# All later products of x taken in the first batch's pauses, and three norms' steps moved to ScalarE

## The reference

```python
x = x + 0.5 * ffn(layernorm(x))        # ffn: sum of 8 chosen adapters, one 256x256 matrix and a bias
x = x + attn(layernorm(x))             # below
x = x + 0.5 * ffn(layernorm(x))
# attn(x): RWKV block
h  = layernorm(x, g1, b1); hh = time_shift(h)
xk, xv, xr = (h * tm + hh * (1 - tm) for tm in (tm_k, tm_v, tm_r))
rwkv = sigmoid(xr @ Wr) * wkv(decay, first, xk @ Wk, xv @ Wv)    # a scan over the 512 tokens
x  = x + rwkv @ Wo
h  = layernorm(x, g2, b2); hh = time_shift(h)
xck, xcr = (h * cm + hh * (1 - cm) for cm in (cm_k, cm_r))
return x + sigmoid(xcr @ Wcr) * (square(relu(xck @ Wck)) @ Wcv)  # hidden size 1024
```

## Time and profile before

| | us |
|---|---|
| median of 3 runs | 461.88 (461.78 to 462.07) |
| the profiled execution, its own time | 462.52 |
| its span in the profile | 460.7 |
| PE busy | 444.5 |
| DVE busy | 394.4 |
| ACT busy | 255.8 |
| POOL busy | 153.9 |

### The profile page before, as it was taken

The page is one execution under the profiler, slowest core; times in us unless marked ns, Lnnn a source line. Parts: engine busy times, 40 slices in busy tenths (PEclk is TensorE's granted clock), DMA queues, the critical chain, the costliest instruction groups (busy, mean ns, idle before and its releaser), DMA issues. The chain is left out here.

```text
span 460.7 us, 6181 instructions
## 1 busy us (share of the span) xinstructions
PE 444.5 (96%) x2120; PEld 352.8 (77%) x2120; DVE 394.4 (86%) x813; ACT 255.8 (56%) x416; POOL 153.9 (33%) x126
## 2 busy tenths in 40 slices
PE   8979989999999999999999999999999999999995
PEld 8755966588759885788668885788678885878884
DVE  3889989999999899989998899979998999866224
ACT  1138466944786267814795287906793387826500
POOL 1424051335141544045242444054332534032010
PEclk9999999999999999999999999999999999999999
DMA  6960001002001100012001200010001000000101
GB/s 213 360 228 2 0 1 46 0 2 91 1 0 48 63 29 1 0 46 92 1 0 46 92 1 1 1 46 1 0 1 46 0 2 0 33 15 1 46 1 46
DMA packets 15953, 18.51 MB, mean 40 GB/s; under 512 B 1066, under 2 KB 13618, under 8 KB 15922
## 3 DMA queue, kind: packets, MB, share of 16 engines
q1 hardware_dynamic: 14522, 17.05, 10.5%
q10 hardware_dynamic: 1400, 1.07, 0.8%
HBM read 13.92 MB, written 4.19 MB: 39 GB/s over the span
## 5 line engine op out<-in xcount | busy, mean ns | idle before, releaser
L379 PE MATMUL pair<-wcv_sb,kk 128*128 128x256 f32 x512 | 114.3, 379 | 0.0
L379 PEld LDWEIGHTS pair<-wcv_sb,kk 128*128 128x128 f32 x512 | 96.8, 190 | 12.6
L1012 POOL TENSOR_TENSOR rstd_x<-vare_x,nhalf 128x4 f32<-128x4 f32 (+1 forms) x25 | 29.7, 1189 | 102.1 <-DVE vare_x L679 101.2
L501 ACT ACTIVATE h<-pair,vec 128x512 f32<-128x512 f32 x16 | 11.6, 775 | 88.8 <-PE pair L265 88.8
L357 PE MATMUL pair<-xck_hi,wck_hi 128*128 128x512 f32 x128 | 56.2, 439 | 1.8 <-ACT kk L542 1.1
L361 PE MATMUL pair<-xck_lo,wck_hi 128*128 128x512 f32 x128 | 50.3, 393 | 0.0
L358 PE MATMUL pair<-xck_hi,wck_lo 128*128 128x512 f32 x128 | 50.0, 391 | 0.0
L542 ACT ACTIVATE kk<-pair 128x512 f32<-128x512 f32 x64 | 37.9, 592 | 15.5 <-PE pair L361 13.7
L1055 POOL TENSOR_SCALAR work<-work,lowest 128x512 f32<-128x512 f32 x16 | 26.6, 1662 | 59.0 <-DVE work L770 59.0
L546 ACT ACTIVATE kk<-kk 128x512 f32<-128x512 f32 x64 | 38.9, 635 | 0.8
L1032 POOL TENSOR_TENSOR x2b<-xs,bias_bc 128x512 f32<-128x512 f32 x15 | 19.2, 1281 | 51.5 <-DVE xs L883 51.5
(11 more groups left out here) (123 smaller groups left out, 918.5 us busy)
## 6 DMA issues: line engine op xcount, KB each, us to landing
x<-in_x_dram SPq DMA_DIRECT2D x8, 512.0 KB, 4.1
xt<-in_xt_dram SPq DMA_DIRECT2D x8, 512.0 KB, 5.3
out_dram<-xs SPq DMA_DIRECT2D x16, 256.0 KB, 2.1
work<-in_ffn_w_dram ACTq DMA_DIRECT2D x4, 256.0 KB, 3.8
work<-in_ffn_w_dram SPq DMA_DIRECT2D x4, 256.0 KB, 4.1
kk<-in_wck_dram SPq DMA_DIRECT2D x1, 1024.0 KB, 11.1
wcv_sb<-in_wcv_dram SPq DMA_DIRECT2D x1, 1024.0 KB, 12.6
wk_sb<-in_wk_dram SPq DMA_DIRECT2D x1, 256.0 KB, 9.3
```

The lines of the kernel that those rows point to most:

```text
L379: last = nc.tensor.matmul(bank_of("kv", e, i)[:, t % TB * C:(t % TB + 1) * C], kk[:, n, tok:tok + P], wcv_sb[:, n, :], start=n == 0, stop= ...
L1012: nc.gpsimd.tensor_tensor(dst, src, power, ALU.pow).then_inc(done, 1)
```

## The change

Eight things change at once.

- The products of x for batches 2 to 7 are taken in the head, where the warm products stood. Their transposed inputs are loaded early into tiles that are unused then (x2b, thc, both xs, and the two xt tiles again). ACT copies the products of these six batches from PSUM to SBUF (`keep_first`), and `add_first` reads them there.
- `stats_x(b)` for b of 2 and more leaves DVE. ACT sums along rows with `accum_out`: four passes for the means, four for the variances. They stand behind `residual_of(f)`.
- `norm_first` for batches 1 and later leaves DVE for ACT, as a scale and a shift; POOL computes the shift. It stands behind the second key relu.
- `mix_r` leaves DVE: ACT scales the difference, and POOL adds h1.
- On DVE `stats_x1(f + 1)` comes behind `key_input_rest(f)`, where before it came ahead of `mix_ck(f)`.
- norm1 and norma become one tile, normed; h1 and h2 become one tile, h.
- On PE, the turning of x1 comes after four key blocks (before: three), and that of xa in the middle of the third quarter of the values.
- On ACT, the key relu and square of block 5 come ahead of the exponentials, and `h1_of` behind relu 3 (before: relu 2).

```diff
+            load_xt(2)
             load_weight("wr", wr_sb[:, :, :], wr)
...
+            load_xt(3)
+            load_xt(4)
+            load_xt(5)
             load_weight("wcr", wcr_sb[:, :, :], wcr)
             load_weight("wcv", wcv_sb[:, :, :], wcv)
             load_x(2)
-            load_xt(2)
-            load_xt(3)
+            load_xt(7)
+            load_xt(6)
...
             turn_x1(0)
-            warm(3, 13)
+            first_product(2)
             front_k(0)
             front_v(0)
             front_r(0)
-            pe.wait_ge(q_done, 2)
-            warm(2, 47)
+            first_product(3)
+            first_product(4)
+            first_product(5)
             output_product(0)
-            pe.wait_ge(t1_done, 2)
-            warm(3, 14)
+            first_product(6)
             turn_xa(0)
-            warm(3, 11)
+            first_product(7)
             for e in range(B):
                 f = e + 1
-                channel_keys(e, (0, 1, 2))
+                channel_keys(e, (0, 1, 2, 3))
                 if has(f):
                     turn_x1(f)
-                channel_keys(e, (3,))
...
                     output_product(f)
-                if has(f + 1):
-                    first_product(f + 1, (0,))
                 channel_values(e, 1)
-                if has(f + 1):
-                    first_product(f + 1, (1,))
+                channel_values(e, 2, range(HB // 2))
                 if has(f):
                     turn_xa(f)
-                channel_values(e, 2)
+                channel_values(e, 2, range(HB // 2, HB))
...
+            def stats_x(b):
+                act.wait_ge(x_loaded[b % X1], 16 * (b // X1 + 1))
+                act.wait_ge(rstd_done["x"], b)
+                act.wait_ge(gated_done, 2 * (b - 1) + 2)
+                for t in range(NT):
+                    nc.scalar.activation(thr.rearrange("p h t -> p (h t)")[:, t * C:(t + 1) * C], x1[b % X1][:, t, :], ACT.Identity, scale=-ROOT / C,
+                                         accum_out=mean_x[:, t:t + 1]).then_inc(means_done, 1)
+                for t in range(NT):
+                    act.wait_ge(means_done, NT * (b - 2) + t + 1)
+                    last = nc.scalar.activation(e_v[:, t // TB, t % TB * C:(t % TB + 1) * C], x1[b % X1][:, t, :], ACT.Square, scale=ROOT, bias=mean_x[:, t:t + 1],
+                                                accum_out=var_x[:, t:t + 1])
+                last.then_inc(vars_done, 1)
+
+            def norm_first(b):
+                act.wait_ge(shiftb_done, b)
+                act.wait_ge(turneda, 2 * (b - 1) + 2)
+                for t in range(NT):
+                    last = nc.scalar.activation(normed[:, t, :], x1[b % X1][:, t, :], ACT.Identity, scale=rboth[:, t:t + 1], bias=shiftb[:, t:t + 1])
+                    if t % TB == TB - 1:
+                        last.then_inc(normed1, 1)
+
+            def keep_first(b):
+                for i in range(BANKS):
+                    act.wait_ge(y1_ps, 2 * b + (BANKS if b >= B - 2 else i + 1))
+                    nc.scalar.activation(tok_bank(y1s[b], i), bank3(bank_of("y1", b, i)), ACT.Copy).then_inc(y1s_done, 1)
...
+            def scaled_difference(f):
+                for c in range(CH):
+                    act.wait_ge(xk_done, 2 * f + c + 1)
+                    act.wait_ge(xv_done, 2 * f + c + 1)
+                    nc.scalar.activation(xr[:, c, :], xr[:, c, :], ACT.Identity, scale=V["tm_r"][:, c:c + 1]).then_inc(scaled_done, 1)
...
+                if has(f + 1):
+                    stats_x(f + 1)
+                if has(f):
                     h2_of(f)
...
             def bias_to_x(b):
-                pool.wait_ge(bn_done["x"], b + 1)
+                pool.wait_ge(*((bn_done["x"], b + 1) if b < 2 else (vars_done, b - 1)))
...
+            def mix_r(f):
+                for c in range(CH):
+                    pool.wait_ge(scaled_done, 2 * f + c + 1)
+                    nc.gpsimd.tensor_tensor(xr[:, c, :], xr[:, c, :], h1[:, c, 0:T], ALU.add).then_inc(xr_done, 1)
```

More of the change, by code:

```diff
@@ L31, in build @@
     X1 = 3
+    ROOT = C ** -0.5
     LAST = B - 1
+    EARLY = range(2, B)
     with ExitStack() as ctx:
@@ L71, in build @@
         xa = sb("xa", [P, NT, C])
-        norm1 = sb("norm1", [P, NT, C])
-        norma = sb("norma", [P, NT, C])
+        normed = sb("normed", [P, NT, C])
         thc = sb("thc", [P, NT, C])
         x2b = sb("x2b", [P, NT, C])
+        y1s = {b: sb(f"y1s_{b}", [P, NT, C]) for b in range(2, B - 2)}
         kinds = ("x", "x1", "xa", "x2")
@@ L266, in turn, with to_tokens @@
                     last.then_inc(filled, 1)
-            def to_tokens(stage, src, w, signal, b, filled, part=range(BANKS)):
-                for i in part:
-                    take(pair_of(stage, b), i, signal, 2 * b + i + 1)
+            def to_tokens(stage, src, w, signal, b, filled, first=0):
+                for i in range(BANKS):
+                    take(pair_of(stage, b), i, signal, 2 * (b - first) + i + 1)
                     for t in range(TB):
@@ L308, in ffn_setup, with first_product @@
                 warm(3, 2)
[L310 removed]
+            def first_product(f):
                 if f == 0:
                     pe.wait_ge(s_ffn, 1)
[L313 to L314 removed]
+                pe.wait_ge(xt_loaded[f], 16)
+                if f in EARLY:
+                    to_tokens("y1", xt_of[f], ffn_t, y1s_done, f, y1_ps, first=EARLY[0])
+                else:
+                    to_tokens("y1", xt_of[f], ffn_t, x1_done, f, y1_ps)
             def turn_x1(f):
[L317 removed]
+                turn("turn_x1", normed, h1_done, f, normed1, turned1)
             def front(name, f, src, w, ready, signal, filled):
@@ L373, in channel_values @@
                     pe.wait_ge(s_wcv, 1)
-                if t % TB == 0:
+                if t % TB == 0 and 0 in part:
                     take(PAIR["kv"], i, kvs_done, 2 * e + i + 1)
-                for n in range(HB):
+                for n in part:
                     if t == 0:
@@ L380, in channel_values @@
                                             start=n == 0, stop=n == HB - 1)
-                if t % TB == TB - 1:
+                if t % TB == TB - 1 and HB - 1 in part:
                     last.then_inc(kv_ps, 1)
@@ L435, in _ @@
                     front_v(f)
-                channel_keys(e, range(some, HB))
+                channel_keys(e, (6, 7))
                 if has(f):
@@ L1076, in _ @@
             pool.wait_ge(s_decay, 2)
+            mix_r(0)
             hold_exponents(0)
```

122 lines of the change are left out of this document (70 added, 52 removed).

## The result

The changed kernel takes 478.64 us (median of 4 runs, 477.19 to 480.46), the kernel before 461.86 (461.78 to 462.07) on the same chip. The ratio is 1.0365, with a 95% interval of 1.0324 to 1.0405: slower by some 17 us, where 19 were forecast. The profiled execution took 480.46, the longest of the four.

What follows compares the result with a forecast made beforehand. PE bounded the loop (51.06 us an iteration); after the change a 53.7 us ring through the norm of x1 would. 77.6 + 322.2 + 80.0 = 479.8, with 1.8 around it 481.6 profiled, 481.0 median; range 459 to 491.

Steps and rivals of the forecast that it cites:

- a ring through the norm of x1: Loop chain through ACT, PE, DVE and POOL back to that norm: 47.3 us before, 53.7 after, above PE's 51.06.
- Six rings: Iterations 0 to 5, each taking a first product's sum, at 53.7 us each: 322.2.
- Span: Start at 77.6, six rings of 322.2 and an end of 80.0: 479.8 us, with 1.8 more around it.
- Piece 3: Key product to output product on PE: 24.3 less one key block of 1.4, so 22.9; rwkv 22.1 behind, hidden.
- Piece 5: POOL's root for the norm of xa waits behind ACT's eight sums: 1.1 us more, between 0.3 and 2.7.
- rival of dear sums: ACT's sums along rows cost 0.2 more for each of eight, rings 1.6 longer: 490.6 us; chance 0.18 (486 and above).
- Piece 6: Norm of xa to statistics of x1, with DVE's adds colliding with POOL's x1 + xa: 10.6 us.
- three of them wait until 4.1: Three of DVE's adds of x1 wait for POOL's 2.36 us sum and end at 5.2 behind the norm's start.
- no collision: DVE's adds and POOL's sum do not collide, ring 50.9: 464.2 us median; chance 0.19 (461 to 470).
- Piece 7: Statistics to norm of x1: statistics 2.2, negm 0.3, root 1.45, shift 0.4, so 4.4 us.
- PE stays the bound: Ring in truth 6 us shorter, so all PE loses is gained: 439.6 us median; chance 0.09 (under 455).

Runs made afterwards that it cites:

- e2: Changed kernel with the norm of x1 back on DVE, behind the mix of xcr: 463.67 us, ratio 1.0052 to the kernel before.
- e7: Changed kernel plus seven warm products of the identity ahead of the key product of batch 1: 478.88 us, ratio 1.0376 to the kernel before.
- e6: As e5, but with mix_r left on ACT and POOL: 462.74 us, ratio 1.0028 to the kernel before.
- e1: Changed kernel with the statistics of x of batches 2 to 7 back on DVE: 474.31 us, ratio 1.0273 to the kernel before.
- e4: Changed kernel with h1 earlier in ACT's queue, straight behind square 1: 475.39 us, ratio 1.0281 to the kernel before.
- g2: As g1, but POOL's sum is not held for DVE's adds of x1: 459.71 us, ratio 0.9949 to the kernel before.
- f3: Changed kernel with DVE's adds of x1 made to wait for POOL's sum of x1 and xa: 483.26 us, ratio 1.0458 to the kernel before.
- f2: Changed kernel with POOL's sum of x1 and xa made to wait for DVE's adds of x1: 477.93 us, ratio 1.0363 to the kernel before.
- e3: Changed kernel with POOL's sum of x1 and xa cut from 1024 columns to 128: 469.01 us, ratio 1.0151 to the kernel before.
- e5: Changed kernel with only the products of x moved; statistics, norm, mix_r and DVE's order as before: 462.43 us, ratio 1.0016 to the kernel before.
- f1: Changed kernel with statistics of x and norm of x1 on DVE, adds and key-input mixes early, POOL's roots moved: 461.76 us, ratio 0.9999 to the kernel before.
- g1: Changed kernel, norm of x1 on DVE, x1 statistics behind the adds, value sum later, POOL's sum held, seven warm products: 449.95 us, ratio 0.9733 to the kernel before.

## Why the prediction was right, point by point

*The frame.* It named a ring through the norm of x1 as the new bound. The ring's 52.92 us against PE's 48.98 show a ring above PE's work, and e2 shows that it was this ring: put the norm back and 15 of the 17 us go. The best test of the sum is e7, where the four adds met POOL's sum as forecast: its rings at full clock took 53.4 to 53.6, against 53.7 predicted.

*The terms of the span.* Key product of batch 1 predicted at 77.6, measured 78.41; the 0.8 were there already at the first key block (66.00 in place of 65.2). Six rings 322.2, measured 320.8 (55.88, 52.81, 53.40, 52.83, 52.93, 52.92). Last key product to the end 80.0, measured 478.7 - 399.18 = 79.5. Span 479.8, measured 478.7. Beside the kernel before, the six rings are 16.9 longer (303.9 there, 74.69 to 378.55), the way from the key product of batch 0 to batch 1 2.2 longer, the start 1.5, and the end 2.7 shorter: 18 in the two profiles. The 1.5 of the start lie within what one profile differs from another (29.3 to 32.3 for that key product).

*The pieces*, from the ring 346.26 to 399.18:

| piece | predicted | measured |
|---|---|---|
| 1 norm of x1 to h1 | 4.2 | 391.51 to 395.63, 4.12 |
| 2 h1 to key product | 3.6 | to 399.18, 3.55 |
| 3 key product to output product | 22.9 | 346.26 to 369.17, 22.91 |
| 4 and 5 output product to norm of xa | 8.0 | to 377.02, 7.85 |
| 6 norm of xa to statistics of x1 | 10.6 | to 386.63, 9.61 |
| 7 statistics to norm of x1 | 4.4 | to 391.51, 4.88 |
| sum | 53.7 | 52.92 |

*Piece 3* came out to 0.01, with rwkv hidden behind PE's work as said, though it was ready 21.4 behind the key product and not 22.1. The key block in it is one that the list of the change does not name: on PE block 5 of the keys now stands ahead of the key product.

*Piece 5* came out for the reasons given. The eight sums end 2.9 behind the start of the output product (3.1 said), POOL's root for xa starts 6.8 behind it (6.9 said). The variance of xa took 1.15 beside POOL's bias add, where the same instruction takes 0.17 in e6, and the prediction did not see that. It cost nothing: it ends at 375.89 and the bias add, behind which the root stands in POOL's queue anyway, at 375.87. The rival of dear sums has no ground: the read-out is an instruction of 0.20, but it overlaps, and the step from one ACTIVATE to the next is 0.40 and 0.49 (368.37 to 368.77, 370.46 to 370.95), no more than the 0.49 that the sum had.

The Trainium skill (ScalarE: Activation LUTs, What ACT_TABLE_LOAD costs) priced the eight at 2.8. The trace agrees for the Identity without pointers (0.41 against an estimated 0.40), not for the eight as they stand, 3.7.

*Piece 6* has a step that failed, though the forecast held: "three of them wait until 4.1". None waited in the changed kernel; POOL was stretched by 1.3. DVE paid 1.45 at xs<-xs,thc and 0.45 at xck (1.86 in place of 1.41, beside POOL's next bias add), 1.9 in all instead of the 2.8 that the prediction had for adds and bias add together. The prediction had the mechanism, and took its side from one row. Five other kernels (e1, e2, e4, e7, g2) show the side that it forecast, 3.77 for the four adds, and e7's piece 6 is 10.25. That the changed kernel went the other way made its rings some 0.6 shorter than e7's, and nothing in the prediction says so. f3 and f2 bound it: 483.26 and 477.93. The rival "no collision" (464.2) is nearest to e3, which measured 469.01 with most of it removed.

*Piece 7*: 0.5 longer. POOL's negm took 0.65 instead of 0.3, beside DVE's mixes.

*What it missed.* The first ring took 55.9, 3 us more than the others. Behind an idle 2.78 the key product ran with a granted clock of 0.50, 6.68 in place of 3.70. The program does not decide it: f2, whose program is the same up to there, ran it in 3.70 behind the same wait, and in e7 too, with warm products, it took 3.70. It is luck that this made up for the later rings, which were 0.7 shorter than said, so that six rings came out near 322.

*A step that the runs refute.* The rival "PE stays the bound" said that a ring 6 us shorter would give 439.6. e5 has nearly the ring of the kernel before and gained nothing: the second ring, through the key inputs, begins to bind as soon as PE's share is gone (50.1 at full clock), and the products behind the wait that it leaves run at half clock in five rings of six. So the misses e5 and f1 say that the prediction's way from ring to gain was incomplete, and that the clock is the larger part: an estimated 7 of e5's 9 us. In g1 both are gone.

## What to carry to other kernels

When work is taken from the engine that bounds, write down every ring that passes through its neighbours, not only the one the change lengthens, and give each its length from the trace; with both rings shortened the kernel gained 12 us, and the changed kernel made a loss of 17 of it, 15 of them because a norm was put into a busy queue. Where a DVE instruction with two SBUF inputs and a POOL instruction can meet, don't leave it to chance who waits: order them with a wait. BN_STATS beside POOL's sum was not stretched (g1), but a TENSOR_SCALAR with one tensor input was (f1's norm, the variance of xa). Where PE waited 1.5 us or more ahead of the keys, the next products often ran at half clock: count the 1.3 to 1.5 us that this added to a ring here to the price of the wait. And compare kernels ring by ring, with the same clock and the same side of a collision, since the totals mix them.

## What the runs showed of the hardware

- *The collision goes one of two ways.* POOL's 1024-column sum begins 0.21 to 0.24 us behind DVE's first add in each of these kernels. In the changed kernel and in four of f1's six iterations DVE passes and POOL takes 3.67; in e1, e2, e4, e7 and g2 one DVE add takes 2.59 and POOL takes 2.46 to 2.49. Within a profile it stayed the same in all iterations but f1's. What decides it is open. The Trainium skill (SBUF — State Buffer, Who interferes with whom) says that whoever issues first has the port for the whole instruction and the other "fully blocks". The changed kernel and those four iterations agree with that for the first add, since DVE began first; the five others, where the later POOL instruction went through and a later add waited, agree if each DVE add counts as an issue of its own, and no run tells why it is not always so.
- *Instructions with one tensor input are stretched too.* A 128x4 TENSOR_SCALAR on DVE took 1.15 in place of 0.17 us beside POOL's bias add and ended with it (375.89 and 375.87); f1's norm of x1 took 2.34 in place of 1.38. BN_STATS beside POOL's 1024-column sum kept its 1.40 in g1.
- *The clock falls after short waits.* Granted clock 0.50, that is 1.2 GHz in place of 2.4, in the stretches 78 to 82 and 129 to 132 of the changed kernel. Ahead of the first PE had stood idle for 2.78 us, ahead of the second for 1.30 and 0.48 with 0.41 of work between them. Behind the same 2.78 the key product took 6.68 or 6.69 in the changed kernel and f3, 5.40 in e3, and 3.70, at full clock, in e1 and f2. Behind waits for the key inputs there was a half-clock stretch in five of six rings of e5 (2.04 to 2.23 us), in four of six of e6 (2.20 to 2.27) and in one of six of e2 (1.60), and in none of g2 (1.09 to 1.41). In f1 it followed PE's wait for the turned x2 (1.55) in four of six. The wait alone does not tell.
- *A sum along rows* is two instructions on ACT, 0.41 and 0.20 for 256 columns, that overlap to a step of 0.40.
